# Attention in a patch-token transformer kernel: key tiles placed by DMA, rotation of three tiles in one go, score blocks cut to the keys they see

## What is computed

```python
h = concat([cls, patches @ W_lin.T + b_lin]) + pos; h = concat([h, txt])        # 16 x 165 x 256
xq, xk, xv = x @ Wq, x @ Wk, x @ Wv     # x = layernorm(h); 16 query heads, 4 key/value heads of 16
xq, xk = rope(xq), rope(xk)
scores = xq . xk / sqrt(16);  masked where |i - j| > 32;  softmax over keys
h = h + (softmax @ xv) @ Wo
h = h + ffn(layernorm(h))    # 8-bit rounded activations, ternary weights, 256 -> 1024,
                             # depthwise conv of 3 tokens, silu, 1024 -> 256
```

## Time and profile before

| | us |
|---|---|
| median of three runs (435.99 to 438.02) | 437.55 |
| the profiled execution, its own time | 435.96 |
| span from first to last instruction in it | 434.2 |
| granted TensorE clock, mean over the span | 0.942 |

### The profile page before, as it was taken

One profiled execution on the slowest core, in us unless ns is written; L12 is line 12 of the kernel. 1 busy time (PEld: TensorE's weight loads), 2 busy tenths in 40 slices (PEclk: granted clock), 3 DMA queues, 4 the chain that ended last, 5 costly groups with the idle time before them and its releaser, 6 DMA issues.

```text
span 434.2 us, 8318 instructions
## 1 busy us (share of the span) xinstructions
PE 357.3 (82%) x2920; PEld 274.9 (63%) x2920; DVE 313.8 (72%) x644; ACT 277.2 (64%) x523; POOL 219.7 (51%) x244
## 2 busy tenths in 40 slices
PE   1683998997999697998997799899998998936533
PEld 1452776776787486667775687688667766824423
DVE  1147548754599766887897689859976997899972
ACT  2240356776788755876976698679757966661812
POOL 2306379698389623994499309961983016010000
PEclk9998899997899989999999999999999999985956
DMA  8671051000000010001000100010001000000011
GB/s 232 154 169 24 19 203 27 1 18 10 2 1 2 2 39 22 18 17 33 2 13 14 33 0 11 17 33 0 19 10 31 2 2 15 20 2 0 0 32 31
DMA packets 17788, 13.86 MB, mean 32 GB/s; under 512 B 10109, under 2 KB 16698, under 8 KB 17747
## 3 DMA queue, kind: packets, MB, share of 16 engines
q1 hardware_dynamic: 16852, 12.18, 10.9%
q10 hardware_dynamic: 895, 1.16, 1.0%
HBM read 7.91 MB, written 2.70 MB: 24 GB/s over the span
## 4 chain that ended last, share of the span: by engine, by line
POOL 37%; PE 27%; DVE 11%; issue 10%; ACT 5%; DMA 5%; SPq 3%; POOLq 0%; ACTq 0%; DVEq 0%
POOL qkr L1064 7%; POOL rsn L1059 5%; POOL rc L1057 5%; POOL shared L1084 5%; POOL qsp L1076 5%; PE bank L1635 3%; POOL qsp L1072 3%; SPq L996 3%; PE bank L1842 2%; PE bank L1821 2%; DMA cst<-in_consts 2%; POOL shared L1092 2%; POOL qsp L1073 2%; PE bank L1736 2%; POOL rs L1035 2%
## 5 line engine op out<-in xcount | busy, mean ns | idle before, releaser
L1190 ACT COPY pT<-bank 94x480 f32<-94x480 f32 x88 | 49.0, 557 | 20.1 <-PE bank L1754 20.0
L1408 DVE TENSOR_REDUCE mx<-bank 120x4 fp32r<-120x376 f32 x88 | 47.2, 542 | 18.2 <-PE bank L1736 18.2
L1736 PE MATMUL bank<-kbd,q_hl 128*120 128x376 f32 x176 | 57.2, 410 | 0.0
L1754 PE MATMUL bank<-cst,pr 120*94 120x120 f32 x352 | 52.1, 270 | 2.7 <-ACT pT L1190 1.7
L1035 POOL TENSOR_TENSOR rs<-ve,half_neg 110x3 f32<-110x3 f32 x16 | 15.4, 962 | 75.2 <-DVE ve L1436 43.5
L1182 ACT ACTIVATE pr<-bank 120x376 f32<-120x376 f32 x88 | 42.7, 488 | 16.2 <-PE bank L1744 15.4
L1226 ACT ACTIVATE shared<-bank,conv 128x330 f32<-128x330 f32 x64 | 39.4, 633 | 12.3 <-PE bank L1822 11.5
L1821 PE MATMUL bank<-xT_hi,w1T 128*128 128x330 f32 x128 | 45.4, 360 | 2.1 <-DVE shared L1491 1.7
L1484 DVE SCALAR_TENSOR_TENSOR shared<-bank,conv,shared 128x328 f32<-128x328 f32 x64 | 35.3, 555 | 13.9 <-ACT shared L1226 13.2
L1754 PEld LDWEIGHTS bank<-cst,pr 120*94 120x94 f32 x352 | 37.6, 126 | 11.0 <-issue 5.2
L1042 POOL TENSOR_SCALAR xn<-h,mv,rs 110x256 f32<-110x256 f32 x21 | 29.0, 1387 | 25.6 <-PE bank L1674 25.1
(11 more groups left out here) (120 smaller groups left out, 854.8 us busy)
## 6 DMA issues: line engine op xcount, KB each, us to landing
out<-h SPq DMA_DIRECT2D x8, 330.0 KB
wn<-in_w SPq DMA_DIRECT2D x2, 1024.0 KB, 6.7
shared<-in_x SPq DMA_DIRECT2D x4, 432.0 KB
vw<-qk SPq DMA_DIRECT2D x40, 23.5 KB
h<-in_txt SPq DMA_DIRECT2D x1, 770.0 KB
wlT<-in_lin SPq DMA_DIRECT2D x1, 768.0 KB, 7.2
h<-tokp SPq DMA_DIRECT2D x14, 36.0 KB
h<-in_txt SPq DMA_DIRECT2D x1, 448.0 KB
```

The source lines that it names most:

```text
L1190: nc.scalar.copy(pT[:, g % 3, :], PT_BANK[0:KW, 0:HKV * QP]).then_inc(p_kept, 1)
L1408: nc.vector.tensor_reduce(mx[:, g % 4, :].bitcast(F32R), S_BANKS[g % 2][0:QP, 0:HKV * KW].rearrange("p (k c) -> p k c", k=HKV), axis=AX.X, ...
L1736: o = nc.tensor.matmul(dst, q_hl[n % 2][:, j * QB:(j + 1) * QB, :].bitcast(F32R), kbd[n % 2][:, part, :, k0:k0 + KW].bitcast(F32R), start= ...
L1754: o = nc.tensor.transpose(PT_BANK[0:KW, kv * QP:(kv + 1) * QP], pr[:, g % 3, kv * KW:(kv + 1) * KW], ident[0:QP, 0:QP])
```

## The change

**Key tiles.** From pair 1 on ACT only copies each transposed part whole to `kT` (2 x 330 columns). SP then places it: `place_k` issues 8 transfers of 16 partitions x 2 x 330, each to its key head's columns of `kbd`. The other entries of `kbd` have to be zero: `kbd[0]` has them from pair 0, where the masked copies stay, and POOL clears `kbd[1]` at the start. The first scores of a pair wait for the 8 transfers (`k_in`) instead of for `k_kept`.

**Rotation.** From pair 1 on `rope` works on all three token tiles in each instruction (`rot`, `swp`, 110 x 960), with one semaphore per step; it waits for the third `qk` tile, and `turn_q` waits for the whole.

**Blocks.** Block j now takes only the keys it sees: widths 62, 92, 94, 94, 78, 94, 78, 94, 94, 92, 62 (sum 934, against 11 x 94 = 1034). The mask is added last and only over the edges on which it is not zero: 618 columns per key head for all blocks (block 5, across both images, in full), against 1034. Maxima, shifts, exponentials, transpositions and contexts get narrower with it.

**Orders.** All tables are new, SP's included: `load_v(3)` stands ahead of `store(0)`, and `load_v(7)` behind `place_k(7)`.

```diff
+            def place_k(n):
+                sp.wait_ge(k_kept, 2 * (n + 1))
+                if n == 1:
+                    sp.wait_ge(kbd_zeroed, 1)
+                else:
+                    sp.wait_ge(scored, NB * (n - 1))
+                for kv in range(HKV):
+                    for at in (HD * kv, QK + HD * kv):
+                        sp.dma_start(kbd[n % 2][at:at + HD, :, kv, :], kT[at:at + HD, :, :]).then_inc(k_in[n % 2], 16)
...
+            nc.gpsimd.memset(kbd[1][:, :, :, :], 0.0).then_inc(kbd_zeroed, 1)
...
             def keep_k(n, part):
                 act.wait_ge(k_turned, 2 * n + part + 1)
-                if n >= 2:
-                    act.wait_ge(scored, NB * (n - 1))
-                for kv in range(HKV):
-                    o = nc.scalar.activation(kbd[n % 2][:, part, kv, :].bitcast(F32R), k_bank(n, part)[:, 0:T], ACT.Copy,
-                                             scale=kvmask[:, kv:kv + 1])
-                o.then_inc(k_kept, 1)
+                if n:
+                    if n == 1:
+                        act.wait_ge(pix_turned, 2 * LOADS)
+                    else:
+                        act.wait_ge(k_in[(n - 1) % 2], K_PLACED * (n // 2))
+                    nc.scalar.copy(kT[:, part, :].bitcast(F32R), k_bank(n, part)[:, 0:T]).then_inc(k_kept, 1)
...
-            def rope(n, t):
+            def rope(n, ts, parts, added, high, split, before):
-                pool.wait_ge(qk_kept, NT * n + t + 1)
+                pool.wait_ge(qk_kept, NT * n + ts.stop)
-                nc.gpsimd.tensor_tensor(rc[:, :].rearrange("p (h d) -> p h d", h=heads), q_v,
-                                        rope_tab[:, t, 0, :].unsqueeze(1).to_broadcast([TT, heads, HD]), ALU.mult)
+                nc.gpsimd.tensor_tensor(rot[:, ts, :].rearrange("p t (h d) -> p t h d", h=heads), q_v, table(0), ALU.mult)
...
             def scores(n, j):
-                    pe.wait_ge(k_kept, 2 * (n + 1))
+                    if n:
+                        pe.wait_ge(k_in[n % 2], K_PLACED * ((n + 1) // 2))
+                    else:
+                        pe.wait_ge(k_kept, 2)
-                nc.tensor.matmul(dst, identb[0:QP, 0:QP], mask_v[:, j, :].unsqueeze(1).to_broadcast([QP, HKV, KW]),
-                                 start=True, stop=False)
                 for part in range(2):
-                    o = nc.tensor.matmul(dst, q_hl[n % 2][:, j * QB:(j + 1) * QB, :].bitcast(F32R),
-                                         kbd[n % 2][:, part, :, k0:k0 + KW].bitcast(F32R), start=False, stop=(part == 1))
+                    nc.tensor.matmul(dst, q_hl[n % 2][:, j * QB:(j + 1) * QB, :].bitcast(F32R),
+                                     kbd[n % 2][:, part, :, k0:k0 + w].bitcast(F32R), start=(part == 0), stop=(part == 1))
+                nc.tensor.matmul(over, identb[0:QP, 0:QP], hide,
+                                 start=False, stop=True, skip_group_check=True).then_inc(scored, 1)
...
     'sp.store': (
-        (8,),
-        (12,),
+        (11,),
+        (15,),
```

More of the change, by code:

```diff
@@ L69, with keys_of, edges @@
 POSR = NPATCH + 1
-def key_start(j):
-    return min(max(QB * j - HALF_WINDOW, 0), T - KW)
+def keys_of(t):
+    lo = t // SEQ * SEQ
+    return max(t - HALF_WINDOW, lo), min(t + HALF_WINDOW + 1, lo + SEQ)
+SEEN = [[keys_of(t) for t in range(QB * j, QB * (j + 1))] for j in range(NB)]
+KEY0 = [min(lo for lo, hi in seen) // 2 * 2 if j < NB // 2 else min(lo for lo, hi in seen) for j, seen in enumerate(SEEN)]
+WIDTH = [-(-(max(hi for lo, hi in seen) - k0) // 2) * 2 for seen, k0 in zip(SEEN, KEY0)]
+def edges(j):
+    lo, hi = max(lo for lo, hi in SEEN[j]) - KEY0[j], min(hi for lo, hi in SEEN[j]) - KEY0[j]
+    if lo >= hi:
+        return 0, 1, WIDTH[j]
+    left, right = lo, WIDTH[j] - hi
+    if not left:
+        return hi, 1, right
+    if not right:
+        return 0, 1, left
+    return 0, 2, max(left, right)
+MASK_AT = [0]
+for _j in range(NB):
+    MASK_AT.append(MASK_AT[-1] + edges(_j)[1] * edges(_j)[2])
 def tok_pieces(s):
@@ L556 @@
+        (403,),
         (),
@@ L710, in times_of @@
         return [(t, k) for k, t in enumerate(ONCE[name])]
-    return [(t, (n, k)) for n in range(PAIRS) for k, t in enumerate(ORDER[name][n]) if t is not None]
+    return [(t, (n, k)) for n, row in enumerate(ORDER[name]) for k, t in enumerate(row) if t is not None]
 TICKS = sorted({t for name in (*ORDER, *ONCE) for t, _ in times_of(name)})
@@ L1007, in _ @@
                     load_v(n)
+                for n, _ in work["place_k"].get(q, ()):
+                    place_k(n)
                 for s in work["move_tok"].get(q, ()):
@@ L1108, in _ @@
                     dequant_x(n)
-                for n, t in work["rope"].get(q, ()):
-                    rope(n, t)
+                for n, _ in work["rope"].get(q, ()):
+                    rope_pair(n)
         @block.scalar
@@ L1169, in keep_k @@
                 act.wait_ge(k_turned, 2 * n + part + 1)
[L1170 to L1175 removed]
+                if n:
[4 more added lines that the diff above has]
+                    nc.scalar.copy(kT[:, part, :].bitcast(F32R), k_bank(n, part)[:, 0:T]).then_inc(k_kept, 1)
+                else:
+                    for kv in range(HKV):
+                        o = nc.scalar.activation(kbd[0][:, part, kv, :].bitcast(F32R), k_bank(0, part)[:, 0:T], ACT.Copy,
+                                                 scale=kvmask[:, kv:kv + 1])
+                    o.then_inc(k_kept, 1)
             def exp(n, j):
@@ L1690, in turn_q @@
             def turn_q(n, t):
-                pe.wait_ge(q_split[t], n + 1)
+                if n:
+                    pe.wait_ge(q_split, n)
+                else:
+                    pe.wait_ge(split_first[t], 1)
                 if n == 0:
```

755 lines of the change are left out of this document (394 added, 361 removed), and 176 rows, old and new, of the table ORDER.

## The result

The changed kernel takes **450.37 us** (median of 4 runs, 448.93 to 452.78) against 437.11 (4 runs, 435.99 to 438.02): ratio **1.031**, 95% interval 1.0258 to 1.0362. Forecast were 425, and 408 to 441. The profiled execution took 450.24, its span 448.4.

A forecast was written before the change was run, and what follows sets the result against it. No engine full; the serial front of the next pair through `F_BANK` sets each pass. 435.96 - 4 (SP) - 26.6 (keys, rotation, blocks) + 18 (key waits, pair 1, pair 7's values) = 423.4, on the median's scale 425 us; range 408 to 441.

The forecast's parts named there:

- the merged rotation: POOL's rotation of three tiles at once: 12.5 us instead of 17.4, later start, net 0.5 us saved per pair.
- I count that as nothing: Longer POOL instructions holding up DVE: taken as no cost; as a rival 6.4 us a pair, 470 us, chance 0.02.
- The 32 rows of PE: PE's work between pair 4's last key transposition and first scores, without scores: covers 8.1 of 10.3 us needed.
- SP's order: Pair 3's loads ahead of pair 0's store shorten one 48 us pass: 4 us saved, bounds 0 and 5.
- Key copies and placement: Two plain ACT copies save 2.7 us per pair; eight DMAs take 8.4 us, costing 13 in waits, 3 in pair 1.
- the six waits of 2.2: PE waits 2.2 us for placed keys at the first scores of pairs 2 to 7: 13 us, bounds nothing and 45.
- Pair 1: Its scores come some 8 us later, some 5 of it slack: cost 3 us, bounds 0 and 8.
- Pair 7's values: Their load stands behind pair 7's key placement in SP's order: about 2 us of waiting, bounds 0 and 8.
- Narrow blocks: Score-sized matmuls stream 2864 fewer columns: PE does 1.3 us less per pair, 0.6 of it on the path.
- The rival on TensorE's pace: Matmuls of 248 columns run at full f32 pace, 0.30 us longer each: 14.6 us, 440 us; chance 0.05.
- Late keys: Placement of 11.7 us makes PE wait 5.5 at each pair's first scores, perhaps lowering the clock: 445 us; chance 0.12.
- The loop through `F_BANK`: Next pair's front, one PSUM bank, `turn_xn` waiting for `k_kept`: sets passes, 8 us longer than the busiest elementwise engine's time.

The follow-up runs named there:

- a_rope1: The changed kernel with the rotation one tile at a time again, each beginning with its own qk copy: 437.05 us.
- a_split: Changed kernel with pair 7's values ahead of its placement, rotation split (tile 0 alone, two merged): 437.95 us, against 432.03 with rotation tile by tile.
- a_2q: Changed kernel with tile-by-tile rotation and pair 7's values ahead of its placement (432.03 us), key DMAs issued four by SP, four by ACT: 451.04 us.

## Why the prediction was wrong

The step that failed is the merged rotation: forecast -0.5 us a pair, measured +13.3 in all. Its times held: 12.5 us on POOL forecast and 12.5 measured (5.6 to 18.1), start 4.5 later forecast and 4.4 measured against before. The 12.5 was in part luck: undisturbed instructions were to take 9.4, by a slope from 160 and 320 columns, and the shortest of each shape add up to 10.8 (480 columns took 1.41, not 1.13); the 3.1 allowed for the rest was 1.7. What failed is the sentence "I count that as nothing" on longer POOL instructions, with a chance of 0.02 and a price of 6.4 us a pair for the rival. The hold-up is real and small, DVE is busy 318.8 us instead of 310.4 in `a_rope1`, 1.2 a pair. It cost more than itself where the held instruction is one that PE's queue stands for: the maximum ahead of `turn_max` above all, and the product L1566 by way of ACT; and the clock fell behind these waits. The medians that I leaned on (L1508 within 0.02 of its lowest) say how often it is hit, not where.

A second step was missing: the new orders had no price of their own, only the waits that they cover. On the old parts they cost 10 us, of which 4.4 are at the end. The 32 rows of PE that were to cover the placement are not free of scores either: row 386 is the last scores of pair 3.

The others, in turn:
- SP's order: -4 forecast, -2.2 measured. Right, too large.
- Key copies and placement: -18.9 + 13 + 3, so -3 net; measured -14.6. An issue took 0.65 (0.76 taken), a landing 2.1 (2.35), so 7.3 us, not 8.4. The failed term is the six waits of 2.2: the rows of 248 columns, which open each pair, waited 4.0 us in the whole program, not 13.

```profile
L1050 SPq DMA_DIRECT2D kbd<-shared x56: 585/593/1745, 77.1 to 344.8; - x56
...
L1808 PE MATMUL bank<-kbd,q_hl 128*120 128x376 f32 x80 | 27.0, 422 | 1.2 <-ACT pr L1250 1.1
...
L1808 PE MATMUL bank<-kbd,q_hl 128*120 128x248 f32 x32 | 7.6, 320 | 4.0 <-issue 3.9
```

- Pair 1: its scores come 3.5 us later (83.8 against 80.3) and pair 2's 3.2 earlier: slack, as argued, and more of it than the forecast's 5.
- Pair 7's values: +2 forecast, +5.0 without merging, +1.2 with it. By the forecast's own figures it is 3.1 (21.5 less 8.4 and 10).
- Narrow blocks: -4.2 forecast, -3.6 in the new order, -1.0 in the old, hardly clear of no change. The rival on TensorE's pace fell: 320 ns at 248 columns, 422 at 376.
- "Late keys", 445 us, named low-clock stretches in the middle. They came, but behind `turn_max` and two waits of the attention, not behind the keys.
- The loop through `F_BANK`, on which the first part rests, did not set the passes after: PE waits for no rotation in the middle, `a_split` ends the rotation sooner and is slower, `a_2q` issues the keys sooner and is slower. In the kernel before, too, PE's queue hardly stood for the rotation from pair 2 on (0.1 us); what waited there for POOL was DVE's `max_x`, 14.2 us, for the `norm2` behind the rotation.

## What to carry to other kernels

When instructions of one engine are merged to save their fixed cost, look at which single instruction of the engine beside it the rest waits for, and what a hold-up of that one by the longest merged instruction costs; a median over all of them hides it. A table of orders is fitted to the parts that it was made for: price it by itself, on the old parts, before any part is credited or blamed. And a wait goes where it is covered: the eight transfers that seemed the dear edit were the one that paid most.
